# Statistics of the two mixtures moved into the run-outs of the attentions before them, and the start of both attentions rearranged

## The reference

```python
x = x + tanh(g_xattn[0]) * L0_xattn(layernorm(x), ctx)    # 16 heads of 8, 120 keys, logits clipped to +-1e4
x = x + tanh(g_ffn[0])   * L0_ffn(layernorm(x))           # 64 experts, top 6 of 4 of 8 groups, and a shared expert
x = x + tanh(g_xattn[1]) * L1_xattn(layernorm(x), ctx)    # 16 heads of 64, 120 keys
x = x + tanh(g_ffn[1])   * L1_ffn(layernorm(x))           # causal latent attention with rope (16 heads of 4), then 8 experts, top 2
```

## Time and profile before

| what | value |
|---|---|
| median of 3 runs (lowest, highest) | 1964.97 us (1957.45, 1966.51) |
| the profiled execution's own time | 1962.93 us |
| its span, first to last instruction | 1961.2 us |
| mean granted TensorE clock | 0.969 of 2.4 GHz |
| busy share of the span: PE, PEld, DVE, ACT, POOL | 92%, 69%, 77%, 60%, 59% |
| front, a_att, b_route, from first instruction to first of the next | 48.3, 206.7, 83.6 us |
| block of projections, dt | 47.1, 221.6 us |

### The profile page before, as it was taken

One profiled execution on the slowest core, in us unless ns is written; L12 is line 12 of the kernel. 1 busy time (PEld: TensorE's weight loads), 2 busy tenths in 40 slices (PEclk: granted clock), 3 DMA queues, 4 the chain that ended last, 5 costly groups with the idle time before them and its releaser, 6 DMA issues. The chain is left out here.

```text
span 1961.2 us, 38316 instructions
## 1 busy us (share of the span) xinstructions
PE 1796.8 (92%) x11886; PEld 1346.0 (69%) x11886; DVE 1512.4 (77%) x3071; ACT 1169.9 (60%) x2993; POOL 1150.5 (59%) x1158
## 2 busy tenths in 40 slices
PE   6888875999999999996999999998889999799998
PEld 4455553788888888863777777776545556588886
DVE  5899977787888787767667777774789996678876
ACT  6466645555555555552677777776556666455554
POOL 4677545676777677643333334433678875667764
PEclk9999987999999999998999999999999997799999
DMA  5111001856565656530000000000000000222222
GB/s 145 33 44 48 27 17 33 166 145 144 131 145 144 144 130 146 129 76 4 5 5 5 5 5 5 1 2 1 1 1 1 0 1 17 79 81 65 81 65 70
DMA packets 99708, 115.17 MB, mean 59 GB/s; under 512 B 18256, under 2 KB 55184, under 8 KB 99568
## 3 DMA queue, kind: packets, MB, share of 16 engines
q1 hardware_dynamic: 98192, 113.16, 23.8%
q10 hardware_dynamic: 1376, 0.30, 0.1%
HBM read 101.76 MB, written 3.28 MB: 54 GB/s over the span
## 5 line engine op out<-in xcount | busy, mean ns | idle before, releaser
L76 POOL TENSOR_TENSOR b_moe_hid_low<-b_moe_hid,b_moe_hid_high 128x512 fp32r<-128x512 f32 x256 | 331.4, 1295 | 173.3 <-ACT b_moe_hid_high L1046 171.4
L1052 ACT ACTIVATE bank<-bank 128x512 f32<-128x512 f32 x384 | 223.5, 582 | 335.5 <-PE bank L83 335.2
L1890 POOL TENSOR_TENSOR XC<-XC,c_recip 128x480 f32<-128x480 f32 x128 | 126.7, 990 | 274.1 <-DVE c_recip L2050 274.0
L1077 DVE TENSOR_TENSOR b_moe_gu<-bank,XC 128x512 f32<-128x512 f32 x256 | 176.7, 690 | 116.0 <-PE bank L83 96.9
L76 POOL TENSOR_TENSOR e_moe_hid_low<-e_moe_hid,e_moe_hid_high 128x512 fp32r<-128x512 f32 x128 | 165.6, 1294 | 84.7 <-ACT e_moe_hid_high L1046 83.8
L2006 ACT ACTIVATE XC<-bank,c_shift 128x120 f32<-128x120 f32 x512 | 177.2, 366 | 19.8 <-DVE c_shift L2040 19.8
L1082 DVE TENSOR_TENSOR b_moe_hid<-bank,b_moe_gu 128x512 f32<-128x512 f32 x256 | 177.0, 691 | 8.9 <-POOL b_moe_hid_low L76 0.3
L71 DVE CAST c_ts_high<-bank 128x480 fp32r<-128x480 f32 x128 | 84.2, 658 | 121.4 <-PE bank L83 120.9
L1046 ACT ACTIVATE b_moe_hid_high<-b_moe_hid 128x512 fp32r<-128x512 f32 x256 | 159.8, 624 | 17.4 <-DVE b_moe_hid L1082 16.8
L2001 ACT ACTIVATE b_YT<-bank 120x512 f32<-120x512 f32 x128 | 76.6, 599 | 104.0 <-PE bank L1938 102.1
L1077 DVE TENSOR_TENSOR e_moe_gu<-bank,XC 128x512 f32<-128x512 f32 x128 | 88.4, 691 | 62.5 <-PE bank L83 51.2
(11 more groups left out here) (398 smaller groups left out, 5656.9 us busy)
## 6 DMA issues: line engine op xcount, KB each, us to landing
XC<-b_comb SPq DMA_DIRECT2D x256, 256.0 KB, 4.5
XC<-e_comb SPq DMA_DIRECT2D x64, 256.0 KB, 3.2
X<-in_x SPq DMA_DIRECT2D x8, 256.0 KB, 6.4
a_att_qs_high<-XC SPq DMA_DIRECT2D x32, 64.0 KB, 1.8
a_att_qs_low<-a_Q_low SPq DMA_DIRECT2D x32, 64.0 KB, 1.8
a_att_ks_high<-a_K_high SPq DMA_DIRECT2D x32, 64.0 KB, 1.8
a_att_ks_low<-a_K_low SPq DMA_DIRECT2D x32, 64.0 KB, 1.9
b_moe_w_gate<-in_b_wgT SPq DMA_DIRECT2D x8, 256.0 KB, 2.9
```

The lines of the kernel that those rows point to most:

```text
L76: return eng.tensor_tensor(low.bitcast(F32R), x, high, ALU.subtract)
L1052: act.activation(gate_b[j % 4][:], gate_b[j % 4][:], ACT.Silu).then_inc(s_silu, 1)
L1077: dve.tensor_tensor(gu[j % 2][:], up_b[j % 2][:], comb[j // 2][:, (j % 2) // share, :], ALU.mult).then_inc(s_gu, 1)
L1890: pool.tensor_tensor(prob[r % 8], prob[r % 8], recip[:, r % 8, :].unsqueeze(2).broadcast_to([P, HG, NKV]), ALU.mult).then_inc(s_norm, 1)
```

## The change

Three things are altered; the computation is the same.

- **Statistics ahead.** A class `Ahead` holds the statistics of a mixture. In rounds NB+1 to NB+4 of each attention DVE runs seven `step`s, two in each of rounds 33 to 35 and one in round 36: the bn_stats of quad k (after a wait for the output of its last block, s_out) and the gathering and variance of quad k-1. POOL takes the roots of quads 0 to 5 in the attention's block, before its casts of ident16 and causal16 in a_att. `settle` is left with the bn_stats of quad 7, the gathering of quads 6 and 7 and two roots, all before its other work; its fillings go from 20 to 8.
- **Attentions begin with scores.** The 20 fillings at the start become 2. In a_att PE's product for the NaN test stands behind the first half of the first scores; DVE still waits for it before its first row maximum.
- **First keys of dt in the block of the projections.** That block becomes the function `project`, handed to `attend_both_ways` as `front`. ACT makes the high parts of blocks 0 and 1 behind quad 3, POOL clears dt's tiles behind quad 2 and spreads the keys of block 0 behind quad 4.

```diff
+            def step(self, dve, k, s_out):
+                if k > 0:
+                    self.gather(dve, k - 1)
+                dve.wait_ge(s_out, 4 * k + 4)
+                self.tiles(dve, k)
+            def rest(self, dve):
+                self.tiles(dve, NQ - 1)
+                self.gather(dve, NQ - 2)
+                self.gather(dve, NQ - 1)
...
                     over_rounds(pool, body, NB + 2)
-                    if front is not None:
+                    ahead.setup(pool)
+                    for q in range(NQ - 2):
+                        ahead.roots(pool, q)
+                    if clamp:
...
-                    keep_busy(pe, out_b, 8)
-                    if clamp:
-                        pe.wait_ge(s_odd, 2)
-                        pe.matmul(side_b[:, 0:1], ones[:], anyodd[:], start=True, stop=True).then_inc(s_oddsum, 1)
-                        pe.wait_ge(s_limit, 1)
-                    keep_busy(pe, out_b, 12)
+                    keep_busy(pe, out_b, 2)
                     pe.wait_ge(s_clear, 2)
...
                             score_phase(t, v, (0, 1), t - 2, (v - 2) % 4, (2, 3)).then_inc(s_first, 1)
+                        if clamp and isinstance(t, int) and t == 0:
+                            pe.wait_ge(s_odd, 2)
+                            pe.matmul(side_b[:, 0:1], ones[:], anyodd[:], start=True, stop=True).then_inc(s_oddsum, 1)
...
+                        if isinstance(t, int) and NB < t <= NB + 3:
+                            ahead.step(dve, 2 * (t - NB) - 2, s_out)
                         if has(t):
                             dve.wait_ge(s_second, t + 1)
...
+                        if isinstance(t, int) and NB < t <= NB + 3:
+                            ahead.step(dve, 2 * (t - NB) - 1, s_out)
+                        if isinstance(t, int) and t == NB + 4:
+                            ahead.step(dve, 6, s_out)
...
-                    keep_busy(pe, bank[6], 20)
+                    keep_busy(pe, bank[6], 8)
...
                     for q in range(NQ):
                         sums(q)
+                        if q == 2:
+                            clear(pool)
+                        if q == 4:
+                            spread_keys(pool, 0, 0)
...
                         centre(q)
+                        if q == 3:
+                            act.wait_ge(s_sum, 2)
+                            high_parts(act, 0, 0)
+                            high_parts(act, 1, 1)
```

More of the change, by code:

```diff
@@ L174, in attend_both_ways @@
+        def attend_both_ways(tag, ctx, Q, K, V, nk, wo, dst, ahead, front, sums=None):
             clamp = sums is not None
@@ L847, in build @@
         own = ExitStack()
-        attend_both_ways("a_att", own, Q, K, V, NKV, small["a_wo"], X, sums, front)
+        ahead = Ahead("b_route", X, True)
+        attend_both_ways("a_att", own, Q, K, V, NKV, small["a_wo"], X, ahead, front, sums)
         own.close()
@@ L1145, in pad_top, with settle @@
             i.then_inc(last_sem, 1)
-        def settle(tag, ctx, src, dst, gain, XT, combD, s_stored, gateT, ne, comb, scores, weights, shared=None):
+        def settle(tag, ctx, src, dst, gain, XT, combD, s_stored, gateT, ne, comb, scores, weights, ahead, shared=None):
             centred = dst is not None
-            bn = sb(f"{tag}_bn", [P, NB, 6], ctx=ctx)
-            mv = sb(f"{tag}_mv", [P, NB, 2], ctx=ctx)
-            var = sb(f"{tag}_var", [P, NB], ctx=ctx)
-            rstd = sb(f"{tag}_rstd", [P, NB], ctx=ctx)
-            shift = sb(f"{tag}_shift", [P, NB], ctx=ctx)
-            root = sb(f"{tag}_root", [P, 4], ctx=ctx)
             if centred:
@@ L1226, in mean_square @@
[L1226 to L1231 removed]
                     def centre(q):
                         if centred:
[L1235 removed]
+                            dve.wait_ge(ahead.s_rs, q + 1)
@@ L1253, in _ @@
+                    for q in range(NQ):
+                        centre(q)
                     dve_scores(dve)
@@ L1256, in _ @@
                 def _(pool):
-                    pool.memset(root[:], -0.5).then_inc(s_root, 1)
+                    ahead.roots(pool, NQ - 2)
+                    ahead.roots(pool, NQ - 1)
                     pool_setup(pool)
-                    pool.wait_ge(s_root, 1)
-                    def roots(q):
-                        part = slice(4 * q, 4 * q + 4)
-                        pool.wait_ge(s_var, q + 1)
-                        pool.tensor_tensor(rstd[:, part], var[:, part], root[:], ALU.pow).then_inc(s_rs, 1)
                     def low_tokens(q):
@@ L1293, in scale @@
                             b = 4 * q + j
-                            i = act.activation(xn[q][:, j, :], src[:, b, :], ACT.Copy, scale=rstd[:, b:b + 1])
+                            i = act.activation(xn[q][:, j, :], src[:, b, :], ACT.Copy, scale=t_rstd[:, b:b + 1])
                         i.then_inc(s_scaled, 1)
@@ L1560, in scalar_behind @@
                     act.activation(YT[:, (t - 3) * 512:(t - 2) * 512], cls.down_b[u], ACT.Copy).then_inc(s_sy, 1)
-        settle("b_route", own, X, XC, None, XT, b_combD, s_stored, small["a_gate"], E0, cw, b_scores, weights, Shared)
+        settle("b_route", own, X, XC, None, XT, b_combD, s_stored, small["a_gate"], E0, cw, b_scores, weights, ahead, Shared)
         own.close()
@@ L2263, in build @@
+        own = ExitStack()
+        ahead = Ahead("e_route", Z, False)
+        attend_both_ways("dt", own, QT, KT, V, P, small["d_up8"], Z, ahead, project)
         own.close()
@@ L2344, in e_scores @@
             return dve_scores, act_scores, pool_scores, act_last, pool_setup, s_lg
-        settle("e_route", own, XC, None, small["g2"], XT, e_combD, s_stored, small["d_router"], E1, ew, e_scores, weights)
+        settle("e_route", own, XC, None, small["g2"], XT, e_combD, s_stored, small["d_router"], E1, ew, e_scores, weights, ahead)
         own.close()
```

418 lines of the change are left out of this document (203 added, 215 removed).

## The result

| what | before | after |
|---|---|---|
| median (lowest, highest) of 13 runs each | 1963.79 us (1957.45, 1967.21) | 1950.95 us (1947.11, 1955.62) |
| the profiled execution, its span | 1962.93, 1961.2 us | 1951.14, 1949.4 us |

The ratio is 0.9937, with a 95% interval of 0.9927 to 0.9947: 12.8 us shorter. The forecast was 1948.0, in the range 1937 to 1958. The profiled execution is 11.8 us shorter than that of before. Both are short of the 15.0 us forecast, and the sum was reached by other terms: one was lost almost whole, and others gave more.

What follows compares the result with a forecast made beforehand. PE was busy 92% of the span, but the prediction examined waits where blocks meet, with DVE's chain setting b_route's end. Terms -3.4 - 6.2 - 2.4 - 3.0 = -15.0 us against 1962.9 gave 1947.9, 1948; range 1937 to 1958.

Steps and rivals of the forecast that it cites:

- a_att's start: First attention's start: first row maximum at 51.0 instead of 54.38, -3.4 us (bounds -4.5 to 0).
- its run-out: End of a_att: added statistics steps, a root and POOL's two casts delay the next block, +3.4 us (+1 to +8).
- b_route: First routing: first routing score 17.7 us after the block's start against 27.3, -9.6; with the run-out's +3.4, -6.2.
- projections and dt: Work moved into the projections costs +1.2, dt's earlier first maximum gains 3.6: together -2.4 us (0 to -5).
- dt's run-out: End of dt: the added statistics steps, without casts, delay the next block by +3.4 us (+1 to +10).
- e_route: Second routing: first router maximum 5.1 us after the start instead of 11.5, -6.4; -3.0 left after the run-out.
- 0, if PE loses its full clock: Bound on the first attention's start: no gain there instead of -3.4 us if PE drops from full clock.
- The prediction's own sign of being wrong: In a_att's first 10 us: a granted clock under 1 would show the prediction wrong.
- The rival of the clock: Attention starts: PE at half clock while the pipeline fills, 2.2 us more per half-round, +20 us, 1983; chance 0.05.
- Three quads go before XT_low begins: Centring in the first routing: three quads at 1.1 us each, then five at 2.5 us beside POOL.
- first routing score near 276: First routing: its first routing score expected near 276 us, with the block starting near 258.3; 282.23 before.
- 2.9 named as a sign of being wrong: First routing: centring taking over 2.9 us a quad would show the prediction wrong; 2.5 was taken beside POOL.

Runs made afterwards that it cites:

- front_filled: The change with 7 fillings more behind PE's last product in the block ahead of the first attention: 1948.89 us, 0.9938 to the kernel before.
- e_short: The change with 3 fillings for 8 at the second routing's start, 12 for 5 behind both run-outs' last product: 1948.47 us, 0.9921 to before.
- stats_alone: The change's statistics in the run-outs alone, both attention starts as before, dt's first keys spread in its own block: 1952.75 us, 0.9955 to before.
- a_start_before: The change with the first attention started as before (8 fillings, test's product, wait, 12 fillings, then scores): 1953.96 us, 0.9958 to before.
- two_left: The change with 5 statistics steps instead of 7 in dt's run-out, POOL's setup ahead of the roots left: 1951.07 us, 0.9938 to before.
- dt_twenty: The change with 20 fillings instead of 2 at the last attention's start: 1953.82 us, 0.9953 to the kernel before.

## Why the prediction was right, and where it was wrong

| step of the sum | forecast | measured in the profiles |
|---|---|---|
| a_att's start | -3.4 | -3.64 at the first maximum, -0.8 at the fifth, +1.3 at the last turn |
| its run-out | +3.4 | +2.55 |
| b_route | -9.6 | -9.4 |
| projections and dt | -2.4 | -3.5 |
| dt's run-out | +3.4 | +2.35 |
| e_route | -6.4 | -5.1 |
| from e_route's last maximum to PE's last instruction | 0 | +0.3 |

With the +1.3 of a_att the steps come to -11.5 us at PE's last instruction, and the span to -11.8, where -15.0 was forecast. That the total lies in the range owes something to luck: 4.7 us less at a_att's start and 1.3 less in e_route stand against 1.9 more in the two run-outs and 1.1 more in dt. In the +1.3 are some 2 us of stretches in the steady rounds, two after against one before, that are not the change's; without them a_att's last turn would stand at -0.8.

**a_att's start is the step that failed.** "I take 51.0 instead of 54.38: -3.4" was right for the first maximum, and the bound "0, if PE loses its full clock" comes near to what happened to the lead, of which 0.8 us is left at the fifth. The prediction's own sign of being wrong, a granted clock under 1 in a_att's first 10 us, came true. Against the clock the prediction said that "a_att enters warm, 8 fillings in 1.89 us". That was a reading of the old program: in it PE also stood still for 1.92 us ahead of the block, but ran 8 fillings behind that gap. With 2 fillings, short products and waits behind the same gap the clock falls; with 7 fillings in the gap it doesn't (front_filled). The rival of the clock was right in its mechanism and wrong in its size: three half-rounds took 0.8 to 1.05 us more each, not 2.2 (DVE's row maximum in them takes 1.16 us at either clock), and the fourth none. The Trainium skill (TensorE: Matmul & The Clock Gate, Part 1) has the array clocked down when it isn't kept busy. The prediction used that rule for dt, where the row of before showed it; the trace of after agrees for a_att, with 0.68 and then 0.50 in 48 to 56 us behind an idle 1.92 us. In the trace of before the same idle stretch is followed by full clock.

**The run-outs** cost less by 0.9 and 1.0. As forecast, the steps that fall beside waiting cost nothing, since the last heads don't move, and the last ones were priced well: the last addition comes 0.90 us later behind the last heads (forecast 0.97), and POOL ends 5.6 us behind them (5.7). In a_att 0.78 of the price is the casts' (0.85). What was too large is the way from there to the next block, from "257.3" to "258.3". In the run-out of before DVE's last addition ended at 253.92, 1.0 us ahead of b_route, but this was not what the block waited for. PE's five fillings ended last:

```profile
253.43 1.24 PE L154 MATMUL bank<-filling 128*128 128x512 bf16 x5
```

From their end at 254.67 it is 0.3 us to the next block, and from the end of POOL's cast at 258.47 in the change as well.

**b_route** was right in size. "Three quads go before XT_low begins": they do, in 3.1 us (forecast 3.3), and the five others take 12.0 (12.5). The "first routing score near 276" came at 275.5, from a block that began 0.5 us later than forecast. But the pace of the five isn't the forecast one of two instructions let through in every quad. Beside POOL they went at 3.4 us a quad (nine in 7.75 us), in that stretch over the 2.9 named as a sign of being wrong, and then ten went free in 2.5 us while POOL waited for ACT's tokens. At the first score the gain is 10.5 us and not 9.6; 1.1 of it is lost by b_route's end. The shared lock of the Trainium skill (SBUF — State Buffer, Who interferes with whom) would have had each of the two roots stop the first centring: the roots run from 260.26 to 262.34, and PE turned the first quad at 261.73, 1.16 us after its centring began at 260.57. The trace does not agree for these small roots: the six centring instructions beside them take 0.34 us each, and a seventh 0.47.

**dt** gained 1.1 us more: 2.3 us from start to first maximum, not 4, since the clock fell only at 1407.9, behind the masks and most of the first products; the prediction had PE cold from the start. **e_route** had its maximum at 6.6 us, not 5.1, because PE was at half clock from about 1626; where it was not (e_short) it came at 5.07. The net of -2.8 is near the -3.0 forecast only because the run-out was cheaper.

## What to carry to other kernels

Work that is moved into a run-out costs only what stands behind the last heads, so move as many steps as fit beside its waits, and leave the last one to the next block if its engine is idle there. Before taking fillings away at a block's start, look at TensorE's idle time at the end of the block before: a few fillings there kept the clock for what follows and cost nothing as long as they didn't end last (0.1 and 0.3 us in the run-outs where they did). When a difference of 1% is made of terms of 1 to 3 us, cut every profile at the same instructions, since the clock moves a single execution by as much.

## What the runs showed of the hardware

- A stretch at 1.2 GHz in the steady rounds of a_att comes at other places in other executions of the same program (73 us in one, 91 and 121 in the other), with PE busy 3.9 to 4.0 of 4 us in it. Over all programs the favoured place is in or just behind the thinnest stretch, 68 to 72 us. From the first row maximum to the last turn, profiles with full clock throughout have 181.2 us (stats_alone, front_filled), those with only the slow start 184.1 and 184.2, and that of the change, with two more stretches, 187.8. The runs of one kernel differ by 4 to 12 us; these falls, at 1 to 2 us each, are a part of that.
- A fall at the start of b_route (PE at half clock for 3.4 us within 256 to 262) stands in a_start_before, two_left and dt_twenty. Their first routing score comes 19.7, 19.7 and 19.1 us behind the start instead of 16.7 to 17.6, and b_route takes 84.4, 85.2 and 82.1 us instead of 80.4 to 81.8 (all with seven steps). What brings it on in some executions only was not tried.
- PE can be "busy" for 4.00 of 4 us and be at half clock; the busy share alone would read as a better filled engine (3.69 and 4.00 after, 3.24 and 3.45 in front_filled).
